# Token-wise attention of a fused transformer kernel: two serial passes of eight tiles become one pipeline of sixteen

## The chip, the cores and the metric

The kernel runs on one core of a Trainium2 chip. The metric is the device time of one launch in microseconds (us). The core has a tensor engine (PE; its weight loads are shown as PEld), a vector engine (DVE), a scalar engine (ACT), GpSimd (POOL) and a sync engine (SP). They run their own instruction streams and meet only in semaphores.

## The reference, cut to what matters

The whole program is a chain of attention, feed-forward and mixture-of-experts layers on a stream of 4 x 512 tokens with 128 features, all in fp32. The change concerns one of them, the first layer of the second block. It is an attention inside one token: the 16 heads of a token attend to each other, with 8 features a head.

```python
# B, S, DM, H = 4, 512, 128, 16
Q = (x @ Wq.T).reshape(b, s, h, hd)
K = (x @ Wk.T).reshape(b, s, h, hd)
V = (x @ Wv.T).reshape(b, s, h, hd)
scores = jnp.einsum('bshd,bstd->bsht', Q, K) / math.sqrt(hd)
attn = jax.nn.softmax(scores, axis=-1)
out = jnp.einsum('bsht,bstd->bshd', attn, V).reshape(b, s, dm)
return out @ Wfc.T
...
x = x + _L1_attn_a_ref(_layernorm(x, axis=-1), Wq, Wk, Wv, Wfc)
```

Each token needs 16 x 16 scores of 8 products each, so a tile of 128 tokens (one token to a partition) has 2048 products to a partition for the scores and 2048 for the values.

## The kernel before

The program is cut into stages, and between two stages all engines meet: each drains and counts up `batch_done`, SP clears the semaphores and counts up `batch_go`. The stage in question is the fifth, called "c" in the code. The windowed attention with its feed-forward part comes before it, the experts after it.

Before the change the stage is a loop over two halves of the stream (`Fori(0, NP)`), of 8 token tiles each (`PAIR`). A half copies its rows from `X` to `XB`, norms them (`layer_norm`, whose inverse root is taken by POOL, L1879), and writes `Y`. PE turns four tiles at a time (L318) and projects them to queries, keys and values, 384 columns a tile (L734); ACT copies these out of PSUM into `c_qkv`. Then DVE goes through the tiles `u`:

- `scores(u)`: the products of queries and keys (L1674, 2048 elements), their sums over the 8 features (L1678), the maximum of each head (L1679), the subtraction (L1680). ACT takes the exponential (L1169).
- `weights(u)`: the sum of the exponentials (L1685), the reciprocal (L1686), the multiplication of the 256 weights (L1687), which releases POOL.
- POOL multiplies weights and values (L2036, 2048 elements).
- `summed(u)`: DVE sums these products over the 16 heads (L1691) into `c_os`.

DVE issues them as scores(u), summed(u-2), weights(u-1). Every DVE step waits for the step before it through `after`. At the end of a half PE turns the sums (L318) and applies the output matrix (L741), and DVE adds the result to the rows (L1707). All tiles of the stage are fp32 and lie in one buffer, `arena`; `small` holds the maxima, sums and reciprocals, `ps` is PSUM with 8 banks.

In the lines printed here, `part` and `full` are views, `tt` is `dve.tensor_tensor`, and `wide` repeats an operand along an axis. `need(engine, sem, n)` waits only if n is above zero.

Of the kernel before, what the change touches and what calls it, by code (L numbers as in the profile page):

```python
# [21 lines left out]
P = 128  # L22
# [89 lines left out]
def program(nc, x_in, w_in, c_in, r_in, out, scratch, c_at):  # L112
# [3 lines left out]
    with ExitStack() as ctx:  # L116
# [35 lines left out]
        def carve(n):  # L152
# [62 lines left out]
        c_qkv = carve(PAIR * 384).rearrange("p (j n) -> p j n", j=PAIR)  # L215
        c_prod = carve(2048)
        c_mix = carve(2 * 2048).rearrange("p (z n) -> p z n", z=2)
        c_sc = carve(2 * 256).rearrange("p (z h t) -> p z h t", z=2, h=HB)
        c_e = carve(2 * 256).rearrange("p (z h t) -> p z h t", z=2, h=HB)
        c_os = carve(PAIR * P)  # L220
        c_oT = carve(512)

# [31 lines left out]
            c_xT_ps c_xT c_proj c_qkv_in c_shift c_exp c_wts c_prod c_red c_sum c_os_in c_oT_ps c_oT_in c_out  # L254
# [58 lines left out]
        def _(pe):  # L313
# [412 lines left out]
            def head_attention(ln):  # L726
                pe.wait_ge(s.ln_out, ln)
                for z in range(2):
                    transposes(0, lambda j: Y[:, NT * z + j, :]).then_inc(s.c_xT_ps, 1)
                    pe.wait_ge(s.c_xT, z + 1)  # L730
                    if z:
                        pe.wait_ge(s.c_qkv_in, z)
                    for j in range(NT):
                        last = mm(ps[:, 1 + j, 0:384], xT[:, j * P:(j + 1) * P], W("c_qkv"), start=True, stop=True)  # L734
                    last.then_inc(s.c_proj, 1)
                for z in range(2):
                    pe.wait_ge(s.c_os_in, z + 1)
                    transposes(0, lambda j: c_os[:, (NT * z + j) * P:(NT * z + j + 1) * P]).then_inc(s.c_oT_ps, 1)
                    pe.wait_ge(s.c_oT_in, z + 1)
                    for j in range(NT):  # L740
                        last = mm(ps[:, 5 + z, j * P:(j + 1) * P], c_oT[:, j * P:(j + 1) * P], W("c_fc"),  # L741
                                  start=True, stop=True)
                    last.then_inc(s.c_out, 1)

# [115 lines left out]
            def stages(which):  # L860
                ln = 0
                for i, st in enumerate(which):
                    if st == "c":
                        ln += 1
                        head_attention(ln)
# [24 lines left out]
            if STAGES >= 5:  # L890
                with pe.Fori(0, NP) as b:
                    pe.wait_ge(batch_go, b + 5)
                    pe.sem_inc(batch_seen, 1)
                    stages(["c"])
                    pe.drain().then_inc(batch_done, 1)
            if STAGES >= 6:
                pe.wait_ge(batch_go, NP + 5)
                pe.sem_inc(batch_seen, 1)
                experts(0)
            if STAGES >= 7:  # L900
                with pe.Fori(0, NB) as b:
                    pe.wait_ge(batch_go, b + NP + 6)
# [3 lines left out]
            if STAGES >= 8:  # L906
                pe.wait_ge(batch_go, NB + NP + 6)
# [7 lines left out]
        def _(act):  # L915
# [243 lines left out]
            def head_attention():  # L1159
                for z in range(2):  # L1160
                    act.wait_ge(s.c_xT_ps, z + 1)
                    copy(xT[:, :], ps[:, 0, :]).then_inc(s.c_xT, 1)
                    act.wait_ge(s.c_proj, z + 1)
                    copy(c_qkv[:, NT * z:NT * z + NT, :], ps[:, 1:1 + NT, 0:384]).then_inc(s.c_qkv_in, 1)
                for u in range(PAIR):
                    act.wait_ge(s.c_shift, u + 1)
                    if u >= 2:
                        act.wait_ge(s.c_prod, u - 1)
                    act.activation(c_e[:, u % 2], c_sc[:, u % 2], ACT.Exp, scale=float(HD) ** -0.5)\  # L1169
                        .then_inc(s.c_exp, 1)  # L1170
                for z in range(2):
                    act.wait_ge(s.c_oT_ps, z + 1)
                    copy(c_oT, ps[:, 0, :]).then_inc(s.c_oT_in, 1)
# [88 lines left out]
            if STAGES >= 5:  # L1262
                with act.Fori(0, NP) as b:
                    act.wait_ge(batch_go, b + 5)
                    act.sem_inc(batch_seen, 1)
                    steps_done.n = 0
                    stages(["c"])
                    act.drain().then_inc(batch_done, 1)
            if STAGES >= 6:
                act.wait_ge(batch_go, NP + 5)  # L1270
# [3 lines left out]
            if STAGES >= 7:  # L1274
                with act.Fori(0, NB) as b:
                    act.wait_ge(batch_go, b + NP + 6)
# [4 lines left out]
            if STAGES >= 8:  # L1281
                act.wait_ge(batch_go, NB + NP + 6)
# [8 lines left out]
        def _(dve):  # L1291
# [374 lines left out]
            def head_attention():  # L1666
                part = lambda u, n: c_qkv[:, u, 128 * n:128 * n + 128].rearrange("p (h d) -> p h d", h=HB)
                full = [P, HB, HB, HD]

                def scores(u):  # L1670
                    b = u % 2
                    dve.wait_ge(s.c_qkv_in, u // NT + 1)
                    prod = c_prod.rearrange("p (h t d) -> p h t d", h=HB, t=HB)
                    after(tt(prod, part(u, 0).unsqueeze(2).broadcast_to(full),  # L1674
                             part(u, 1).unsqueeze(1).broadcast_to(full), ALU.mult))
                    if u >= 2:
# [648 lines left out]
```

## Time and profile before

| | us |
|---|---|
| median of the runs before (2257.24 to 2271.3) | 2269.24 |
| the profiled execution, its own time | 2261.32 |
| its span, first to last instruction | 2259.5 |
| stage "c" within it, from 1566.18 to the first instruction of the next stage at 1802.24 | 236.06 |

Over the span PE is busy 72%, DVE 58%, ACT 48% and POOL 39%, and TensorE's granted clock is 0.846 of full speed. These are means over eight stages with different limits; what this change does is read from its own stage.

### The profile page before, as it was taken

The numbers are of one execution on the slowest core, as the hardware profiler recorded it, in microseconds if no ns is written. First come the engines' busy times: TensorE is split into PE (matmuls) and PEld (weight loads), VectorE is DVE, ScalarE is ACT, GpSimd is POOL, SyncE is SP. The second block draws the span as 40 slices with busy tenths as digits, with TensorE's granted clock in tenths as the row PEclk, the third lists the DMA queues.
The fourth block names the chain that finished last, engine by engine and source line by source line (L and its number), as shares of the span: only waits on it lengthen the run. The fifth ranks groups of instructions, "written<-read, shape, count | busy, mean of one in ns | idle before, by whom it ended". The sixth has DMA issues, their size and how long they took to land. (4 is left out here: it accounts for less than half of the span.)

```text
span 2259.5 us, 37774 instructions
## 1 busy us (share of the span) xinstructions
PE 1630.8 (72%) x13344; PEld 1160.5 (51%) x13344; DVE 1318.2 (58%) x3740; ACT 1083.2 (48%) x2727; POOL 874.8 (39%) x628
## 2 busy tenths in 40 slices
PE   6999996889988568988868998884011166455586
PEld 5888883666666333445436666662010055344464
DVE  3454545886776245567568777752968745433344
ACT  3565664877787245654347778762000022222132
POOL 1232234766665013244366666640544402100102
PEclk9999998999999868998779999997555578777578
DMA  4000000111111000000001111100000001000001
GB/s 178 1 1 1 1 1 12 30 27 24 28 30 22 6 0 1 1 1 2 1 20 27 27 26 29 24 20 5 0 0 0 0 1 38 0 0 0 0 4 53
DMA packets 31073, 36.43 MB, mean 16 GB/s; under 512 B 19120, under 2 KB 21168, under 8 KB 30512
## 3 DMA queue, kind: packets, MB, share of 16 engines
q1 hardware_dynamic: 29872, 32.01, 5.4%
q8 instruction: 106, 1.74, 0.3%
q0 software_dynamic: 1024, 2.10, 0.3%
q14 instruction: 71, 0.58, 0.1%
HBM read 12.08 MB, written 3.15 MB: 7 GB/s over the span
## 5 line engine op out<-in xcount | busy, mean ns | idle before, releaser
L918 ACT ACTIVATE arena<-ps 128x512 f32<-128x512 f32 (+5 forms) x684 | 373.8, 606 | 297.9 <-PE ps L318 143.1
L318 PE MATMUL ps<-consts,arena 128*128 128x128 f32 x416 | 89.1, 362 | 296.4 <-DVEq L1695 139.8
L318 PEld LDWEIGHTS ps<-consts,arena 128*128 128x128 f32 x416 | 61.1, 181 | 328.1 <-DVEq L1695 141.6
L1053 ACT ACTIVATE arena<-arena,g_small 128x128 f32<-128x128 f32 x512 | 199.0, 404 | 0.5
L1153 ACT ACTIVATE arena<-ps 128x320 f32<-128x320 f32 (+4 forms) x256 | 132.5, 561 | 137.4 <-PE ps L676 134.6
L1460 DVE CUSTOM_DVE_ANT_0 arena<-ps,consts,g_ss 128x128 f32<-128x128 f32 x512 | 145.6, 347 | 77.1 <-PE ps L482 72.2
L1962 POOL TENSOR_TENSOR arena<-arena,consts 128x512 f32<-128x512 f32 (+1 forms) x64 | 92.9, 1452 | 194.3 <-ACT arena L1153 194.2
L1983 POOL TENSOR_TENSOR arena<-arena 128x512 f32<-128x512 f32 x64 | 82.1, 1282 | 183.8 <-DVE arena L1468 183.7
L2036 POOL TENSOR_TENSOR arena<-arena 128x2048 f32<-128x2048 f32 x16 | 109.5, 6842 | 99.9 <-DVE arena L1687 99.9
L676 PE MATMUL ps<-arena 32*128 32x160 f32 (+4 forms) x1024 | 119.9, 454 | 21.1 <-ACT arena L1153 10.5
L1879 POOL TENSOR_TENSOR rstd<-rstd,consts 128x4 f32<-128x4 f32 (+2 forms) x16 | 28.8, 1798 | 262.4 <-DVE rstd L1317 219.9
L1467 DVE TENSOR_TENSOR arena<-ps,tabs 128x512 f32<-128x512 f32 x128 | 87.7, 685 | 50.7 <-ACT arena L1022 44.8
L1993 POOL TENSOR_TENSOR g_ss<-g_ss,consts 128x8 f32<-128x8 f32 x64 | 105.4, 1647 | 7.1
L1805 DVE SCALAR_TENSOR_TENSOR arena<-ps,arena 128x128 f32<-128x128 f32 x256 | 72.1, 344 | 61.8 <-PE ps L850 60.3
L1402 DVE TENSOR_REDUCE arena<-arena 128x8 f32<-128x1032 f32 x32 | 39.3, 1228 | 115.7 <-ACT arena L976 115.7
L583 PE MATMUL ps<-arena,weights 128*128 128x512 f32 (+1 forms) x192 | 101.4, 639 | 6.0 <-ACT arena L1082 4.1
L676 PEld LDWEIGHTS ps<-arena 32*128 32x128 f32 x1024 | 60.8, 204 | 87.4 <-ACT arena L1153 53.9
L1996 POOL TENSOR_TENSOR g_ss<-g_ss,consts 128x8 f32<-128x8 f32 x64 | 104.7, 1636 | 0.0
L1053 ACT ACTIVATION_READ_ACCUMULATOR arena<-arena,g_small 128x1 f32 x512 | 103.8, 203 | 0.0
L1909 POOL TENSOR_TENSOR arena<-arena,consts 128x8 f32<-128x8 f32 x32 | 52.6, 1645 | 124.2 <-DVE arena L1402 124.2
L2052 POOL DMA_INDIRECT sorted_rows<-arena,e_idx x32 | 30.9, 967 | 169.6 <-DVE arena L1805 162.3
L1986 POOL TENSOR_TENSOR arena<-arena 128x512 f32<-128x512 f32 x64 | 81.4, 1271 | 38.8 <-issue 35.2
(249 smaller groups left out, 4287.2 us busy)
## 6 DMA issues: line engine op xcount, KB each, us to landing
arena<-arena SPq DMA_DIRECT2D x112, 128.0 KB, 2.3
weights<-in_w SPq DMA_DIRECT2D x1, 5069.0 KB, 24.0
weights<-in_w SPq DMA_DIRECT2D x1, 2052.0 KB, 12.5
arena<-Y SPq DMA_DIRECT2D x16, 128.0 KB
arena<-Y SPq DMA_DIRECT2D x16, 127.0 KB
consts<-in_c SPq DMA_DIRECT2D x1, 1278.0 KB, 8.6
out<-X SPq DMA_DIRECT2D x1, 1024.0 KB, 5.1
sorted_rows<-arena,e_idx POOLq DMA_INDIRECT x32
```

The costliest lines, as they stand in the source:

```text
L318: last = tr(ps[:, bank, j * P:(j + 1) * P], src(j), ident)
L583: mm(ps[0:m, 4 + c % 2, :], W("f_w1", at, at + m), g_hnT, start=True, stop=True)\
L676: last = mm(ps[:, 2 * (st % 2) + hh, 0:n], b_kT[rows, k % 2, r, j * P:(j + 1) * P], b_qT[rows, k % 2, j * P:j * P + n], start=True, stop=True)
L918: copy = lambda o, i: act.activation(o, i, ACT.Copy)
L1053: last = act.activation(g_p[:, n % 2, 4 * hf + i, :], g_sc[:, 4 * hf + i, :], ACT.Exp, scale=-1.0, bias=g_mn[:, h:h + 1], accum_out=g_rs[: ...
L1153: act.activation(b_p[:, U % 2, 2 * gp:2 * gp + 2, at:at + n], ps[:, b:b + 2, 0:n], ACT.Exp, scale=float(HD) ** -0.5).then_inc(s.b_exp, 1)
L1460: last = dve.tensor_tensor_reduce(g_sc[:, 4 * hf + i, :], ps[:, 4 + hf, i * P:(i + 1) * P], C("mask_f" if n % NT else "mask_f0"), g_ss[:, ...
L1467: tt(heads(low[0]), heads(src), table(tabs_at), ALU.mult)
L1962: pool.tensor_tensor(v, v, m.unsqueeze(1).broadcast_to([P, NG, n]), ALU.mult)\
L1993: stepped_after(pool.tensor_tensor(ss[:, 8:16], ss[:, 8:16], C("neghalf", 0, 8), ALU.pow))
L1996: pool.tensor_tensor(ss[:, 0:8], ss[:, 0:8], C("neghalf", 0, 8), ALU.pow).then_inc(gs.root, 1)
L2036: pool.tensor_tensor(c_mix[:, u % 2].rearrange("p (h d t) -> p h d t", h=HB, t=HB), c_e[:, u % 2].unsqueeze(2).broadcast_to(full), vals.un ...
```

## The change

The loop over halves is gone; one pipeline goes over the 16 tiles of the stream (`TT`), and norms four tiles at a time as it comes to them, straight from `X`. For each tile:

- The queries stay in PSUM. ACT copies only keys and values (256 columns) to `c_kv`.
- DVE's product (`products`, L1707 of the new file) reads queries from PSUM and keys from SBUF, and writes them feature by feature: 8 planes of 256.
- PE adds the 8 planes: 8 matmuls of 256 columns with the identity as weights, accumulated in PSUM (`sum_products`, L740). The maximum and the subtraction (`shift`) read PSUM.
- The weights are no longer divided. POOL multiplies the exponentials as they are with the values. DVE sums these into PSUM (L1734) and multiplies the 128 sums by the reciprocals (L1735).
- DVE's order is products(t), sums(t-1), values(t-2), shift(t), and at some steps four rows of norm or the addition of an output.

```diff
             def head_attention():
-                part = lambda u, n: c_qkv[:, u, 128 * n:128 * n + 128].rearrange("p (h d) -> p h d", h=HB)
-                full = [P, HB, HB, HD]
-
-                def scores(u):
-                    b = u % 2
-                    dve.wait_ge(s.c_qkv_in, u // NT + 1)
-                    prod = c_prod.rearrange("p (h t d) -> p h t d", h=HB, t=HB)
-                    after(tt(prod, part(u, 0).unsqueeze(2).broadcast_to(full),
-                             part(u, 1).unsqueeze(1).broadcast_to(full), ALU.mult))
-                    if u >= 2:
-                        dve.wait_ge(s.c_exp, u - 1)
-                    after(dve.tensor_reduce(c_sc[:, b], prod, AX, ALU.add))
-                    after(dve.tensor_reduce(mxa[:, :], c_sc[:, b], AX, ALU.max))
-                    tt(c_sc[:, b], c_sc[:, b], wide(mxa[:, :], [P, HB, HB], 2), ALU.subtract).then_inc(s.c_shift, 1)
...
+                heads = lambda ap: ap.rearrange("p (h d) -> p d h", h=HB)
+                full = [P, HD, HB, HB]
+
+                def products(u):
+                    dve.wait_ge(s.c_kv, u + 1)
+                    need(dve, s.c_s, u - 1)
+                    tt(c_prod[:, u % 2].rearrange("p d (h t) -> p d h t", h=HB),
+                       heads(ps[:, u % 2, 0:128]).unsqueeze(3).broadcast_to(full),
+                       heads(c_kv[:, u % 4, 0:128]).unsqueeze(2).broadcast_to(full), ALU.mult).then_inc(s.c_prod, 1)
+
+                def shift(u):
+                    dve.wait_ge(s.c_s, u + 1)
+                    need(dve, s.c_mix, u - 1)
...
+                    sc = ps[:, 2 + u % 2, 0:256].rearrange("p (h t) -> p h t", h=HB)
+                    after(dve.tensor_reduce(mxa[:, :], sc, AX, ALU.max))
+                    tt(c_e[:, u % 2], sc, wide(mxa[:, :], [P, HB, HB], 2), ALU.subtract).then_inc(s.c_shift, 1)
+
+                def sums(u):
+                    r = c_sums[:, u % 2, :]
                     dve.wait_ge(s.c_exp, u + 1)
...
+                    after(dve.tensor_reduce(r, c_e[:, u % 2], AX, ALU.add))
+                    dve.reciprocal(r, r).then_inc(s.c_sum, 1)
+
+                def values(u):
+                    z, j = u // NT, u % NT
+                    dve.wait_ge(s.c_mix, u + 1)
+                    dve.wait_ge(s.c_sum, u + 1)
...
+                    red = ps[:, 7, 0:P]
+                    need(dve, s.c_os, u)
+                    after(dve.tensor_reduce(red, c_mix[:, u % 2].rearrange("p (n t) -> p n t", t=HB), AX, ALU.add))
+                    tt(c_os[:, z % 2, j, :].rearrange("p (h d) -> p h d", h=HB), red.rearrange("p (h d) -> p h d", h=HB),
+                       wide(c_sums[:, u % 2, :], [P, HB, HD], 2), ALU.mult).then_inc(s.c_os, 1)
+
+                for t in range(-5, TT + 4):
+                    if 0 <= t < TT:
+                        products(t)
+                    if 0 <= t - 1 < TT:
+                        sums(t - 1)
+                    if 0 <= t - 2 < TT:
+                        values(t - 2)
+                    if 0 <= t < TT:
+                        shift(t)
+                    z, r = (t + 5) // NT, (t + 5) % NT
+                    if z < NB and r == 0:
+                        norm_stats(0, X[:, NT * z:NT * z + NT, :])
+                        norm_var(0)
+                    if z < NB and r == 1:
+                        norm_apply(0, Y[:, NT * z:NT * z + NT, :], X[:, NT * z:NT * z + NT, :], gs.ln)
+                    if t >= 7 and (t - 7) % NT == 0:
+                        z = (t - 7) // NT
+                        x = X[:, NT * z:NT * z + NT, :]
+                        dve.wait_ge(s.c_out, z + 1)
+                        tt(x, x, ps[:, 6, :].rearrange("p (j d) -> p j d", j=NT), ALU.add).then_inc(s.c_add, 1)
```

PE and POOL, cut to the new parts (PE's loop is turn_x, project(t+1), sum_products(t), rows_out):

```diff
+                def project(u):
+                    z, j = u // NT, u % NT
+                    pe.wait_ge(s.c_xT, z + 1)
+                    need(pe, s.c_prod, u - 1)
+                    mm(ps[:, u % 2, 0:384], c_xT[:, z % 2, j * P:(j + 1) * P], W("c_qkv"), start=True, stop=True)\
+                        .then_inc(s.c_qkv, 1)
+
+                def sum_products(u):
+                    pe.wait_ge(s.c_prod, u + 1)
+                    need(pe, s.c_shift, u - 1)
+                    for d in range(HD):
+                        last = mm(ps[:, 2 + u % 2, 0:256], ident, c_prod[:, u % 2, d, :], start=d == 0, stop=d == HD - 1)
+                    last.then_inc(s.c_s, 1)
...
+                def mix(u):
+                    pool.wait_ge(s.c_exp, u + 1)
+                    need(pool, s.c_os, u - 1)
...
+                for t in range(-5, TT + 1):
+                    z, r = (t + 5) // NT, (t + 5) % NT
+                    if 0 <= t - 1 < TT:
+                        mix(t - 1)
+                    if z < NB and r == 0:
+                        pool.wait_ge(gs.var, rooted.next())
+                        pool.tensor_tensor(g_rstd[:, 0, :], g_rstd[:, 0, :], C("neghalf", 0, NT), ALU.pow)\
+                            .then_inc(gs.root4, 1)
```

DVE in the middle of a half, before (one tile, from its query-key product to the next one):

```order
L1674 TENSOR_TENSOR arena<-arena 128x2048
L1678 TENSOR_REDUCE arena<-arena 128x256
L1679 TENSOR_REDUCE small<-arena 128x16
L1680 TENSOR_TENSOR arena<-arena,small 128x256
L1691 TENSOR_REDUCE arena<-arena 128x128
L1685 TENSOR_REDUCE small<-arena 128x16
L1686 RECIPROCAL small<-small 128x16
L1687 TENSOR_TENSOR arena<-arena,small 128x256
L1674 TENSOR_TENSOR arena<-arena 128x2048
```

DVE now, at step t = 4, the tile after which four rows of the third group are normed (L1377 is the application of the norm, four instructions):

```order
L1707 TENSOR_TENSOR arena<-ps,arena 128x2048
L1724 TENSOR_REDUCE c_sums<-arena 128x16
L1725 RECIPROCAL c_sums<-c_sums 128x16
L1734 TENSOR_REDUCE ps<-arena 128x128
L1735 TENSOR_TENSOR arena<-ps,c_sums 128x128
L1717 TENSOR_REDUCE small<-ps 128x16
L1718 TENSOR_TENSOR arena<-ps,small 128x256
L1377 TENSOR_SCALAR Y<-X,mv,g_rstd 128x128 x4
L1707 TENSOR_TENSOR arena<-ps,arena 128x2048
```

The reduction of 2048 products (L1678) and the product with the reciprocals (L1687) are gone from between two query-key products, and a product of 128 elements (L1735) has come; the subtraction stands last, right ahead of the norm where there is one.

PE before, one half:

```order
L318 MATMUL ps<-consts,Y 128x128 x4
L734 MATMUL ps<-weights,xT 128x384 x4
L318 MATMUL ps<-consts,Y 128x128 x4
L734 MATMUL ps<-weights,xT 128x384 x4
L318 MATMUL ps<-consts,arena 128x128 x4
L741 MATMUL ps<-weights,arena 128x128 x4
```

PE now, from the start of the stage:

```order
L319 MATMUL ps<-consts,Y 128x128 x4
L733 MATMUL ps<-weights,arena 128x384 x2
L740 MATMUL ps<-arena,consts 128x256 x8
L319 MATMUL ps<-consts,Y 128x128 x4
L733 MATMUL ps<-weights,arena 128x384
L740 MATMUL ps<-arena,consts 128x256 x8
L733 MATMUL ps<-weights,arena 128x384
L740 MATMUL ps<-arena,consts 128x256 x8
```

The projections, which stood in two blocks ahead of a half, now stand one by one, each ahead of the 8 matmuls that add the products of a tile.

## Rows read from the trace of the kernel before

**Rows 1.** Stage "c": length, busy us of PE, PEld, DVE, ACT, POOL; clock, DMA share, GB/s.
```profile
1566.18:1802.24 236.06, 31.58 (x96) 20.22 (x96) 180.38 (x186) 19.18 (x30) 112.76 (x18) 0.55 0.00 0
```

**Rows 2.** Timeline of one period of a half: start, length, engine, line.
```profile
1604.63 7.34 POOL L2036 TENSOR_TENSOR arena<-arena 128x2048 f32<-128x2048 f32 x1 [3.87 <-DVE arena L1687]
1606.79 2.29 DVE L1678 TENSOR_REDUCE arena<-arena 128x256 f32<-128x2048 f32 x1
1609.11 0.42 DVE L1679 TENSOR_REDUCE small<-arena 128x16 f32<-128x256 f32 x1
1609.57 2.69 DVE L1680 TENSOR_TENSOR arena<-arena,small 128x256 f32<-128x256 f32 x1
1612.18 2.27 DVE L1691 TENSOR_REDUCE arena<-arena 128x128 f32<-128x2048 f32 x1
1612.29 0.42 ACT L1169 ACTIVATE arena<-arena 128x256 f32<-128x256 f32 x1 [10.80 <-DVE arena L1680]
1614.60 0.42 DVE L1685 TENSOR_REDUCE small<-arena 128x16 f32<-128x256 f32 x1
1615.06 0.25 DVE L1686 RECIPROCAL small<-small 128x16 f32<-128x16 f32 x1
1615.34 0.43 DVE L1687 TENSOR_TENSOR arena<-arena,small 128x256 f32<-128x256 f32 x1
1615.68 2.29 DVE L1674 TENSOR_TENSOR arena<-arena 128x2048 f32<-128x2048 f32 x1
1615.85 7.35 POOL L2036 TENSOR_TENSOR arena<-arena 128x2048 f32<-128x2048 f32 x1 [3.87 <-DVE arena L1687]
```

**Rows 3.** Timeline of the end of the second half.
```profile
1788.59 5.33 POOL L2036 TENSOR_TENSOR arena<-arena 128x2048 f32<-128x2048 f32 x1 [3.71 <-DVE arena L1687]
...
1798.26 2.08 PE L741 MATMUL ps<-weights,arena 128*128 128x128 f32 x8 [0.69 <-ACT arena L918]
1800.37 0.69 DVE L1707 TENSOR_TENSOR XB<-XB,ps 128x512 f32<-128x512 f32 x1 [3.19 <-PE ps L741]
```

**Rows 4.** DVE lines of other stages: count, shortest/median/longest ns, first and last start.
```profile
L1467 DVE TENSOR_TENSOR arena<-ps,tabs x128: 676/682/693, 367.4 to 1489.4; 128x512 f32<-128x512 f32 x128
L1495 DVE RECIPROCAL g_small<-g_small x64: 189/190/203, 395.6 to 1516.3; 128x8 f32<-128x8 f32 x64
L1343 DVE TENSOR_SCALAR Y<-X,mv,g_rstd x64: 333/341/1361, 13.0 to 1242.1; 128x128 f32<-128x128 f32 x64
```

**Rows 5.** Timeline in the second windowed stage: four norm instructions of DVE, one POOL product.
```profile
1240.41 1.80 DVE L1343 TENSOR_SCALAR Y<-X,mv,g_rstd 128x128 f32<-128x128 f32 x3
...
1240.58 1.31 POOL L1983 TENSOR_TENSOR arena<-arena 128x512 f32<-128x512 f32 x1 [1.23 <-DVE arena L1468]
```

**Rows 6.** Matmuls by line and shape: busy us, mean ns of one record.
```profile
L422 PE MATMUL ps<-arena 128*128 128x256 f32 x64 | 19.0, 379 | 0.0
```

**Rows 7.** Timeline: PE in the second half's projections, and in the experts' stage.
```profile
1692.95 5.43 PE L734 MATMUL ps<-weights,xT 128*128 128x384 f32 x8 [0.69 <-ACT xT L918]
...
1863.00 1.02 PE L841 MATMUL ps<-arena,weights 128*128 128x512 f32 x2
```

**Rows 8.** Timeline of the start of the first half.
```profile
1566.91 1.64 DVE L1312 BATCH_NORM_STATS2 stats<-XB 128x6 f32<-128x128 f32 x8
...
1569.51 1.65 POOL L1879 TENSOR_TENSOR rstd<-rstd,consts 128x8 f32<-128x8 f32 x1 [26.59 <-DVE rstd L1317]
1571.19 2.14 DVE L1320 TENSOR_SCALAR Y<-XB,mv,rstd 128x128 f32<-128x128 f32 x8 [1.76 <-POOL rstd L1879]
1573.39 1.12 PE L318 MATMUL ps<-consts,Y 128*128 128x128 f32 x4 [8.46 <-DVE Y L1320]
...
1575.20 4.58 PE L734 MATMUL ps<-weights,xT 128*128 128x384 f32 x8 [0.69 <-ACT xT L918]
```

**Rows 9.** PE's busy time and granted clock in 2 us stretches of the small heads' stage.
```profile
1004.00:1006.00 2.00, 0.48 (x8) 1.00 0.00 0
1006.00:1008.00 2.00, 1.06 (x10) 1.00 0.00 0
```

More of the change, by code:

```diff
@@ L742, in head_attention @@
                                   start=True, stop=True)
                     last.then_inc(s.c_out, 1)
+                for t in range(-3, TT + 3):
+                    z = (t + 3) // NT
+                    if (t + 3) % NT == 0 and z < NB:
+                        turn_x(z)
+                    if 0 <= t + 1 < TT:
+                        project(t + 1)
+                    if 0 <= t < TT:
+                        sum_products(t)
+                    if t >= 6 and (t - 6) % NT == 0:
+                        rows_out((t - 6) // NT)
@@ L890, in _ @@
             if STAGES >= 5:
[L891 to L895, printed above, removed]
+                pe.wait_ge(batch_go, 5)
+                pe.sem_inc(batch_seen, 1)
+                head_attention()
+                pe.drain().then_inc(batch_done, 1)
             if STAGES >= 6:
-                pe.wait_ge(batch_go, NP + 5)
+                pe.wait_ge(batch_go, 6)
                 pe.sem_inc(batch_seen, 1)
@@ L1159, in head_attention, with keep_kv, exps @@
             def head_attention():
[L1160 to L1165, printed above, removed]
-                    act.wait_ge(s.c_shift, u + 1)
-                    if u >= 2:
[L1168 to L1173, printed above, removed]
+                def keep_kv(u):
+                    act.wait_ge(s.c_qkv, u + 1)
+                    need(act, s.c_mix, u - 3)
+                    copy(c_kv[:, u % 4, :], ps[:, u % 2, 128:384]).then_inc(s.c_kv, 1)
+                def exps(u):
+                    act.wait_ge(s.c_shift, u + 1)
+                    act.activation(c_e[:, u % 2], c_e[:, u % 2], ACT.Exp, scale=float(HD) ** -0.5).then_inc(s.c_exp, 1)
+                for t in range(-3, TT + 3):
+                    z = (t + 3) // NT
+                    if (t + 3) % NT == 0 and z < NB:
+                        act.wait_ge(s.c_xT_ps, z + 1)
+                        need(act, s.c_qkv, NT * (z - 1))
+                        copy(c_xT[:, z % 2, :], ps[:, 4, :]).then_inc(s.c_xT, 1)
+                    if 0 <= t + 1 < TT:
+                        keep_kv(t + 1)
+                    if t >= 6 and (t - 6) % NT == 0:
+                        z = (t - 6) // NT
+                        act.wait_ge(s.c_oT_ps, z + 1)
+                        need(act, s.c_out, z)
+                        copy(c_oT, ps[:, 5, :]).then_inc(s.c_oT, 1)
+                    if 0 <= t < TT:
+                        exps(t)
             def full_attention():
@@ L1262, in _ @@
             if STAGES >= 5:
[L1263 to L1268, printed above, removed]
+                act.wait_ge(batch_go, 5)
+                act.sem_inc(batch_seen, 1)
+                steps_done.n = 0
+                head_attention()
+                act.drain().then_inc(batch_done, 1)
             if STAGES >= 6:
-                act.wait_ge(batch_go, NP + 5)
+                act.wait_ge(batch_go, 6)
                 act.sem_inc(batch_seen, 1)
@@ L2161, in _ @@
             if STAGES >= 5:
-                with sp.Fori(0, NP) as b:
-                    sp.wait_ge(batch_done, 4)
-                    clear()
+                sp.wait_ge(batch_done, 4)
+                clear()
             if STAGES >= 6:
```

138 lines of the change are left out of this document (54 added, 84 removed).

## The prediction

> **What bounds the kernel now.** I read the stage's busy times first. Stage "c" lasts 236.1 us; DVE is busy 180.4 us of it, POOL 112.8, PE 31.6 [rows 1]. DVE looks like the bound at 76%, but part of its busy time is waiting. That shows in the timeline of one period [rows 2]: POOL's product L2036 starts at 1604.63 and the next at 1615.85, so a tile costs 11.2 us. Within it POOL and DVE's two-input steps take turns. L1680 is a subtraction of 256 elements; its like L1687 takes 0.43 us, but L1680 takes 2.69 and ends as POOL ends (1612.26 against 1611.97). The product L2036 takes 5.33 us where DVE has nothing to do [rows 3] and 7.34 here, because it starts while L1674 still runs. The reductions L1678 and L1679 run beside POOL at full speed (2.29, 0.42). So a DVE instruction with two SBUF inputs and a POOL product exclude each other, a reduction does not. The loop of waits is: weights (L1687) -> POOL waits for L1674, then works -> L1680 can end -> L1691, L1685, L1686, L1687. POOL itself is idle 3.87 us of the 11.2.
>
> Which DVE instructions are exempt decides much of the change. L1467, a product with one input in PSUM, never takes over 0.69 us in 128 instances, and L1495, a reciprocal, never over 0.20 in 64, in stages in which POOL works beside them. But the norm's L1343, which reads SBUF alone, goes from 0.34 to 1.36 us [rows 4]. How it happens is seen in the timeline [rows 5]: POOL slips in between two of the four instructions of a norm, and the next one waits until POOL is done (three of them take 1.80 us).
>
> **One step of the new pipeline.** DVE's own work: product 2.29 (as L1674, same size), sum of exponentials 0.42, reciprocal 0.25, value sums 2.29 (as L1691), product with the reciprocals about 0.30 (estimated from 0.69 for 512 and 0.43 for 256 elements), maximum 0.42, subtraction 0.42: 6.4 us, some 6.2 with the overlap of independent neighbours (L1674 starts 0.09 before L1687 ends) [rows 2, 3]. The reduction L1678 (2.29), the product L1687 (0.43) and the wait in L1680 (2.27) are gone.
>
> PE's new work is 8 fp32 matmuls of 256 columns. A record of 256 columns takes 0.379 us [rows 6], two overlapping ones of 512 take 1.02 [rows 7]; from the two, a column costs 0.835 ns and the tail of a burst 0.165 us. Each matmul is two records (L734: 4 matmuls, x8), so 16 records at 0.214 are 3.4 us, with the tail 3.6. At the lower clock L734's eight records of 384 took 5.43 us [rows 7]: 1.71 ns a column, twice as much, and 16 records of 256 take 7.0 with their tail.
>
> The step's path: product 2.29, to PE 0.06 (L1320 ends 1573.33, L318 starts 1573.39 [rows 8]), sums 3.6, back 0.05, maximum and subtraction 0.8: 6.8 us. Between product and maximum DVE does 3.3 us of other work, so it waits 0.3 for PE; PE is the bound by a little. Behind that wait stands the next product, and PE waits for that one: the two engines take turns on the path. POOL: its exponentials come 0.55 us after the subtraction (ACT 0.42, and two hand-overs), its product takes 5.33 and must be done when values(t) begins, 6.8 + 3.0 us after that subtraction: 4 us of slack. All DVE products of the step have a PSUM input, so I price the exclusion within a step at nothing; if it were not so, POOL would start 2.3 us late and the reciprocal, if it too had to wait, would stand until 7.6 us into the step; with the value sums and shift() behind it, that is an 11.2 us step. ACT's copy of keys and values is off the path, one step ahead. On PE, the projection (two records of 384, 0.8) and every fourth step the turning of the rows and the output matrix (about 2.3 with ACT's copy) fit into the 3.2 us between PE's end and the next product's end; without that cover they cost up to 2.3 us, three times.
>
> **The sum**, from the start of the stage:
> - To the first product: statistics of four tiles, half of 2.60 (from L1312 to L1879); inverse root 1.65; norm 1.1; turning 1.12; ACT's copy 0.6; projection at the lower clock 1.3 and its tail; ACT 0.4; hand-overs [rows 8]. 8.0.
> - 16 steps of 6.8: 108.8.
> - Norms within the pipeline: statistics after t = 3 and 7 (1.4 each), application after t = 0, 4, 8 (1.1 each): 6.1. Additions at t = 7, 11, 15, 0.7 each [rows 3]: 2.1.
> - **Port stalls**: each application stands right behind shift(t). POOL is released 0.55 us after the subtraction, as the third of four norm instructions runs. As before [rows 5] the next one then waits for the whole POOL product: 5.33 less what runs beside it, 5.2, three times: 15.6. The bounds are 0 (POOL comes after the fourth has begun) and 16.5.
> - [...] A burst that begins after a rest keeps that level for long: the eight projections of one half took 5.43 us [rows 7], those of the other 4.58 [rows 8]. So in the one the clock rose only at the end, in the other some 3.7 us into the burst, 5.5 after the turning had begun. I take 5 us: 2.5 us worth of work is done by then, the remaining 0.9 at full rate; 5.9 instead of 3.4, so 2.5 a restart. Restarts: the first tile, and the one behind each stall (over 9 us of rest): 4 x 2.5 = 10.0. Within steady steps PE rests 2.4 us and works 4.2. The clock stayed full through 4 us with 1.54 busy in another stage [rows 9]; I take the full level here.
> - Tail: after the last subtraction POOL is done at 5.95, value sums and product 2.6, turning 1.2, copy 0.65, output matrix 2.1, addition 0.7 [rows 3, 8]: 13.3; to the next stage 0.4.
>
> Together 164.3 against 236.1: 71.8 less. The profiled execution's own time is 2261.3, so 2189.5; the median of the runs stands 7.9 above that execution. I take half of it: **2193**.
>
> [...] The change reads queries and keys with a step of 8 elements, 32 bytes; before, both were read in rows of 8 neighbours. The row nearest to it is POOL's: L2036 reads the values with that step already and takes 5.33 us for 2048 elements [rows 3], 2.6 ns each, as L1983, which reads runs of 32 neighbours, takes 1.31 for 512 [rows 5]. So POOL pays nothing for it here; DVE has no such SBUF read in the trace. If DVE paid, I bound it by nothing below and POOL's 5.33 above.
> [...]
>
> **Rivals.**
> 1. *The lower clock stays* (17%). The steady burst is short, with a rest in each step. A step is then 2.29 + 0.06 + 7.0 + 0.05 + 0.8 = 10.2; 16 of them cost 54 more, the 10 of restarts fall away: 2237. For it: the stage's 0.55 now. Against it: the stretch that kept the full clock [rows 9], and that at the lower clock PE would work over 8 of 10.2 us, which should lift it; so a mixture, near 2215, is as likely as the whole.
> 2. *No stalls* (17%). The four norm instructions are through before POOL asks (they start 0.27 apart, 1.1 in all; POOL asks at 0.55, so it needs luck). 15.6 and three restarts (7.5) fall away: 2170.
> 3. *The stepped reads are slow* (13%). At 4.5 us a product, between the bounds, a step is 9.0: +35, 2228; at 5.33 it is 2242.
> 4. *The exclusion holds for PSUM inputs and reciprocals too* (3%): steps of 11.2 us, +70, stalls and restarts partly inside: 2250. The lines that never stretch speak against it [rows 4].
> 5. *Slower than before* (3%): the accumulating matmuls do not overlap, each record waits for the tail of the one before, at the lower clock. 16 x (0.43 + 0.17) = 9.6, a step of 12.8; 16 of them are 205 and 45.5 for the rest without restarts: 250, 14 more than now and 86 more than forecast: 2279. It decides from a step of 11.9 us on, that is 8.7 us of PE. Against it: records overlap [rows 6, 7].
> That the change does not do what it says is shut out by the order of instructions.
>
> **Chances.** Forecast 47%, from 2178 to 2212 with the uncertain terms (stalls, restarts, 0.3 us a step). For 8 in 10 the range must take in rivals 2 and most of 1 and 3: 2160 to 2240. A measurement of this kernel tells about 1% (23 us) from no change. Faster by over 1% is all but rival 5, part of 4 and the ends of 1 and 3: 0.95; within 1% 0.03; slower 0.02.
>
> **What the new profile would show.** Right: a period of 6.8 us between DVE's 2048-element products, with DVE waiting some 0.3 us for PE before the maximum; the subtraction at 0.42 us, never 2.7; POOL's product at 5.33 throughout; the norm application stretched to over 6 us at t = 0, 4, 8; a granted clock near 1 between them; 164 us for the stage, other stages unchanged. Wrong: a product over 2.3 us (rival 3), PE's burst at 7 us throughout (rival 1), no norm instruction over 0.4 us (rival 2). What I may have missed: a cost of writing value sums to PSUM (no such DVE write in the trace; priced as L1691), and DVE's extra waits on semaphores, five ahead of the value sums, priced at nothing because they stand behind running work; each tenth of a microsecond there costs 1.6 us.

## The result, and the profile after

| | before | after |
|---|---|---|
| median of 4 runs each, same chip (us) | 2270.27 (2257.24 to 2275.85) | 2242.86 (2237.58 to 2247.2) |
| the profiled execution, its own time | 2261.32 | 2247.2 |
| stage "c" in it | 236.06 | 209.45 |
| everything else in its span | 2023.4 | 2035.9 |

The changed kernel takes 0.9898 of the time before, 95% interval 0.9867 to 0.9929: 23 us less, between 16 and 30. The prediction was 76 less, and the time lies just above the range that was given. The stage itself became 26.6 us shorter; 71.8 were forecast. What surrounds the stage was not changed. It varies in single executions of the kernels of this study between 2013 and 2046 us, so I read the mechanism from the stage, and kernels against each other from their medians.

The stage as a whole, and one steady step cut into pieces (columns as in [rows 1]):

```profile
1562.20:1771.65 209.45, 116.30 (x352) 85.28 (x352) 150.17 (x169) 17.54 (x41) 91.14 (x20) 0.73 0.00 0
1607.50:1611.60 4.10, 0.00 (x1) 0.00 (x0) 4.10 (x3) 0.69 (x2) 3.29 (x1) 1.00 0.00 0
1611.60:1612.60 1.00, 0.99 (x5) 0.89 (x6) 0.97 (x3) 0.00 (x0) 1.00 (x1) 0.99 0.00 0
1612.60:1613.60 1.00, 1.00 (x4) 0.82 (x3) 1.00 (x1) 0.00 (x0) 1.00 (x1) 0.50 0.07 16
1613.60:1614.60 1.00, 1.00 (x4) 0.82 (x3) 0.96 (x2) 0.00 (x0) 0.15 (x1) 0.50 0.00 0
1614.60:1615.60 1.00, 1.00 (x4) 0.73 (x4) 0.06 (x1) 0.00 (x0) 0.00 (x0) 0.50 0.00 0
1615.60:1616.60 1.00, 1.00 (x5) 0.86 (x4) 0.00 (x0) 0.00 (x0) 0.00 (x0) 0.81 0.00 0
1616.60:1617.60 1.00, 1.00 (x4) 0.40 (x3) 0.51 (x2) 0.00 (x0) 0.00 (x0) 1.00 0.00 0
```

PE rests 4.10 us with the clock granted in full, starts its burst in full, and has worked for about a microsecond when the granted clock goes to half (0.50 of full speed). It comes back only toward the end of the burst. The slices hold some 3.4 us at the lower level (three whole ones, and 0.4 of the one that reads 0.81); half of that is 1.7, which is what this burst of 5.41 us takes over the one of 3.72 us in the same stage. The same step in the timeline, from one product of DVE to the next burst of PE (it answers to [rows 2]):

```profile
1597.54 3.85 DVE L1707 TENSOR_TENSOR arena<-ps,arena 128x2048 f32<-128x2048 f32 x1
...
1601.45 5.41 PE L740 MATMUL ps<-arena,consts 128*128 128x256 f32 x16 [4.10 <-DVE arena L1707]
...
1606.90 0.42 DVE L1717 TENSOR_REDUCE small<-ps 128x16 f32<-128x256 f32 x1 [2.41 <-PE ps L740]
1607.36 0.42 DVE L1718 TENSOR_TENSOR arena<-ps,small 128x256 f32<-128x256 f32 x1
1607.70 3.86 DVE L1707 TENSOR_TENSOR arena<-ps,arena 128x2048 f32<-128x2048 f32 x1
...
1608.31 5.45 POOL L2088 TENSOR_TENSOR arena<-arena 128x2048 f32<-128x2048 f32 x1 [4.70 <-ACT arena L1192]
...
1611.61 5.41 PE L740 MATMUL ps<-arena,consts 128*128 128x256 f32 x16 [4.11 <-DVE arena L1707]
```

L1707 is now the query-key product. The ring is the forecast one: product, burst, maximum and subtraction, next product. Its size is not: the product takes 3.86 us where 2.29 was forecast, the burst 5.41 where 3.6 was. The step is 10.16 us, not 6.8. By line over the whole stage (columns: busy us, mean ns of one, idle before):

```profile
L740 PE MATMUL ps<-arena,consts 128*128 128x256 f32 x256 | 90.0, 528 | 54.3 <-DVE arena L1707 54.3
L2088 POOL TENSOR_TENSOR arena<-arena 128x2048 f32<-128x2048 f32 x16 | 87.2, 5447 | 95.1 <-ACT arena L1192 95.1
...
L1707 DVE TENSOR_TENSOR arena<-ps,arena 128x2048 f32<-128x2048 f32 x16 | 61.7, 3856 | 2.6 <-ACT arena L942 2.6
L1734 DVE TENSOR_REDUCE ps<-arena 128x128 f32<-128x2048 f32 x16 | 36.2, 2265 | 2.2 <-POOL arena L2088 2.2
...
L1717 DVE TENSOR_REDUCE small<-ps 128x16 f32<-128x256 f32 x16 | 6.8, 425 | 47.1 <-PE ps L740 47.1
```

DVE idles 47.1 us of the stage for PE, and PE 54.3 us for DVE: neither is the bound, they take turns. Of the 16 bursts, seven take 5.41 us, seven between 5.7 and 6.6, one 5.22, one 3.72; together 90.0. The sum of the prediction had 16 x 3.6 + 10 for restarts, 67.6. The norm at t = 4:

```profile
1629.21 6.12 DVE L1377 TENSOR_SCALAR Y<-X,mv,g_rstd 128x128 f32<-128x128 f32 x4
...
1629.82 5.43 POOL L2088 TENSOR_TENSOR arena<-arena 128x2048 f32<-128x2048 f32 x1 [3.98 <-ACT arena L1192]
```

Four instructions that take 1.12 us at the start of the stage take 6.12, because POOL's product begins between two of them. This happens three times, as forecast.

### The profile page after: what moved, and what is told of

Its sections match the earlier page's. It is cut to its first block and busy times, and to the rows that moved or that the text cites. A ratio compares the mean times of both kernels' runs of the same rounds, so it can differ in the third digit from the quotient of the medians.

```text
span 2245.4 us, 38321 instructions
## 1 busy us (share of the span) xinstructions
PE 1731.9 (77%) x13600; PEld 1238.6 (55%) x13600; DVE 1285.8 (57%) x3722; ACT 1081.9 (48%) x2738; POOL 855.0 (38%) x630
## 3 DMA queue, kind: packets, MB, share of 16 engines
q0 software_dynamic: 1024, 2.10, 0.3%
## 5 line engine op out<-in xcount | busy, mean ns | idle before, releaser
L942 ACT ACTIVATE arena<-ps 128x512 f32<-128x512 f32 (+4 forms) x700 | 376.4, 595 | 327.7 <-PE ps L319 173.5
L2031 POOL TENSOR_TENSOR arena<-arena 128x512 f32<-128x512 f32 x64 | 82.1, 1283 | 183.5 <-DVE arena L1502 183.5
L740 PE MATMUL ps<-arena,consts 128*128 128x256 f32 x256 | 90.0, 528 | 54.3 <-DVE arena L1707 54.3
L2088 POOL TENSOR_TENSOR arena<-arena 128x2048 f32<-128x2048 f32 x16 | 87.2, 5447 | 95.1 <-ACT arena L1192 95.1
L1927 POOL TENSOR_TENSOR rstd<-rstd,consts 128x4 f32<-128x4 f32 (+1 forms) x14 | 25.5, 1822 | 240.0 <-DVE rstd L1351 197.6
L740 PEld LDWEIGHTS ps<-arena,consts 128*128 128x128 f32 x256 | 68.9, 275 | 80.5 <-DVE arena L1707 65.8
L1855 DVE SCALAR_TENSOR_TENSOR arena<-ps,arena 128x128 f32<-128x128 f32 x256 | 72.1, 344 | 61.7 <-PE ps L875 60.8
L319 PE MATMUL ps<-consts,Y 128*128 128x128 f32 x128 | 26.1, 340 | 100.1 <-DVE Y L1354 56.5
```

The costliest lines, as they stand in the source:

```text
L319: last = tr(ps[:, bank, j * P:(j + 1) * P], src(j), ident)
L740: last = mm(ps[:, 2 + u % 2, 0:256], ident, c_prod[:, u % 2, d, :], start=d == 0, stop=d == HD - 1)
L942: copy = lambda o, i: act.activation(o, i, ACT.Copy)
```

## The experiments

The theory behind them: (A) the product is slow because it reads the keys in SBUF with a step of 8 elements, and the longer product is also what makes PE rest long enough to lose its clock; (B) PE's clock would fall anyway, since bursts are short; (C) the product is slow because one input is in PSUM. Each kernel is the changed one with the edit shown. "Stage" is the length of "c" in its profiled execution.

| kernel | edit | median us (runs) | over before, same chip, 95% | stage us | product us | PE bursts, sum us |
|---|---|---|---|---|---|---|
| changed | – | 2242.86 (4) | 0.9898 (0.9867–0.9929) | 209.45 | 3.86 | 90.0 |
| perm | queries and keys feature-major | 2204.05 (4) | 0.9758 (0.9720–0.9795) | 165.73 | 2.28 | 71.5 |
| perm_k | keys only | 2193.88 (1) | – | 174.72 | 2.28 | 80.5 |
| norm_early | norm ahead of the subtraction | 2216.47 (4) | 0.9808 (0.9776–0.9841) | 186.24 | 3.86 | 84.9 |
| fill8 | PE kept busy behind its burst | 2226.23 (4) | 0.9856 (0.9792–0.9920) | 194.33 | 3.87 | 70.8 |
| perm_delay | perm, DVE 1.64 us later | 2220.31 (1) | – | 205.45 | 2.28 | 86.2 |
| k_step4 | keys with a step of 4 | 2238.82 (1) | – | 213.57 | 4 x 1.06 | 91.8 |
| k_step2 | keys with a step of 2 | 2200.52 (1) | – | 171.83 | 2 x 1.22 | 76.5 |
| perm_norm | perm and norm_early | 2175.45 (4) | 0.9620 (0.9579–0.9662) | 148.19 | 2.28 | 72.1 |
| ahead | product(t+1) ahead of the subtraction(t) | 2194.57 (5) | 0.9677 (0.9642–0.9713) | 159.48 | 3.88 | 71.5 |
| perm_norm_ahead | all three | 2151.4 (4) | 0.9504 (0.9461–0.9547) | 133.35 | 2.29 | 64.4 |

### The layout of queries and keys: perm and perm_k

The columns of the two weight matrices are laid out on the host in the order feature, head. Every feature of the 16 heads is then 16 neighbours, and the results are the same numbers.

```diff
+                rows = lambda ap: ap.rearrange("p (d h) -> p d h", h=HB)
...
-                       heads(ps[:, u % 2, 0:128]).unsqueeze(3).broadcast_to(full),
-                       heads(c_kv[:, u % 4, 0:128]).unsqueeze(2).broadcast_to(full), ALU.mult).then_inc(s.c_prod, 1)
+                       rows(ps[:, u % 2, 0:128]).unsqueeze(3).broadcast_to(full),
+                       rows(c_kv[:, u % 4, 0:128]).unsqueeze(2).broadcast_to(full), ALU.mult).then_inc(s.c_prod, 1)
...
-        "c_qkv": side([c["Wq"].T, c["Wk"].T, c["Wv"].T]), "c_fc": c["Wfc"].T,
+        "c_qkv": side([c["Wq"].T.reshape(D, HB, HD).transpose(0, 2, 1).reshape(D, D), c["Wk"].T.reshape(D, HB, HD).transpose(0, 2, 1).reshape(D, D), c["Wv"].T]), "c_fc": c["Wfc"].T,
```

> The columns of the query and key weights are laid out feature by feature on the host, so that the product (L1707 of the changed kernel) reads both operands in runs of neighbours; nothing else changes. Theory: the step of 8 elements costs the product 1.57 us (3.86 instead of 2.29). Then the product is 2.29 us again, PE is released 1.57 us earlier in each of 16 steps, and stage c falls from 209.4 us by up to 25, to about 184. Rival: it is the PSUM operand or the sheer size that makes it slow; then the product stays at 3.86 and the stage at 209. Second rival: the step pays it back to PE, because a shorter step changes nothing in PE's clock or makes it worse: product at 2.29 but the stage at 195 or more.

In perm_k only the keys (the line with `c_kv` and the columns of `Wk`) are changed; the queries in PSUM are still read with a step of 8, each of them 16 times in a row.

> Only the keys are laid out feature by feature; the queries are still read from PSUM with the step, each of them repeated 16 times. Theory: what costs is a new address with every element, and only the keys have that, so the product is 2.29 us as with both. Rival: a step in PSUM costs as well, or the two add up: a product between 2.4 and 3.86.

The timeline of perm at three of its steps, then its product (count, shortest/median/longest ns, first and last start), then the same line of perm_k:

```profile
1608.63 2.28 DVE L1708 TENSOR_TENSOR arena<-ps,arena 128x2048 f32<-128x2048 f32 x1
...
1610.96 3.72 PE L740 MATMUL ps<-arena,consts 128*128 128x256 f32 x16 [2.53 <-DVE arena L1708]
...
1642.58 3.72 PE L740 MATMUL ps<-arena,consts 128*128 128x256 f32 x16 [2.53 <-DVE arena L1708]
...
1680.82 5.41 PE L740 MATMUL ps<-arena,consts 128*128 128x256 f32 x16 [2.53 <-DVE arena L1708]
```
```profile
L1708 DVE TENSOR_TENSOR arena<-ps,arena x16: 2277/2280/2291, 1577.7 to 1715.2; 128x2048 f32<-128x2048 f32 x16
```
```profile
L1708 DVE TENSOR_TENSOR arena<-ps,arena x16: 2278/2279/2293, 1574.7 to 1721.2; 128x2048 f32<-128x2048 f32 x16
```

With rows of neighbours the product is back at 2.28 us, a PSUM input or not, so (C) falls. The keys alone do it: the step of the queries in PSUM costs nothing here. PE now rests 2.53 us ahead of a burst in a steady step. Eight of the 16 bursts take 3.72 us, where the changed kernel had one, and the step is then 6.89; the other eight take 4.78 to 5.53 us, two of them after the same rest of 2.53 us. The stage is 43.7 us shorter than in the changed kernel: 16 x 1.575 = 25.2 from the product and 90.0 - 71.5 = 18.5 from the bursts, together 43.7. Only the 25 had been expected, the bursts had not. Their share is the less certain one: perm_k has the same product and the same rests, but its bursts add up to 80.5 us instead of 71.5, and its stage is 9.0 us longer. So in single executions of one schedule the bursts can differ by as much as that.

### What makes PE's clock fall: fill8 and perm_delay

fill8 leaves the stepped read as it is and gives PE something to do behind each burst, eight matmuls into a corner of PSUM that nobody reads:

```diff
                     last.then_inc(s.c_s, 1)
+                    for _ in range(8):
+                        mm(ps[:, 5, 0:256], ident, W("c_qkv", 0, 256), start=True, stop=True)
```

> PE gets 8 more matmuls of 256 columns behind the sums of each tile, into a bank that is free then, with constant operands; their results are not used. Theory: the clock falls in the middle of each burst (PE rests 4.1 us before it), and a fuller PE keeps it: a burst of 16 records takes 3.6 us in steady steps instead of 5.4, the granted clock of the stage rises from 0.73 to over 0.9, and the stage falls by 13 times 1.8, to about 186, if the filler (3.4 us) fits into PE's rest. Rival: the burst is slow for another reason (accumulation, or the read of the products beside DVE and POOL): bursts stay at 5.4 and the stage at 209 or more.

```profile
1611.49 0.40 DVE L1726 TENSOR_REDUCE c_sums<-arena 128x16 f32<-128x256 f32 x1
1611.61 3.72 PE L740 MATMUL ps<-arena,consts 128*128 128x256 f32 x16 [0.69 <-DVE arena L1709]
```

The slow product stays (3.87 us), the burst takes 3.72 and the step 8.5. The medians of the two kernels are too close to part them (the intervals of the ratios overlap), so this is read from the stage: it gets 15.1 us shorter although PE has twice as many of these matmuls to do, and lies 28.6 above perm, of which the product is 25.4. Eleven of its 16 bursts take 3.6 or 3.7 us, and PE rests 0.69 us ahead of them in a steady step. The bursts give back 19.2 us and the stage only 15.1 (some 186 us had been expected): at three tiles PE turns the sums and applies the output matrix, and there the filler delays the next burst by 0.9 to 1.5 us behind its product. perm_delay is the opposite: the product is fast, and a reduction of 1440 constants, which nobody uses, makes DVE later by what the stepped read had cost.

```diff
+                    dve.tensor_reduce(small[:, 4, :], W("a_qkv", 0, 16 * 90).rearrange("p (n t) -> p n t", t=90), AX, ALU.add)
                     tt(c_prod[:, u % 2].rearrange("p d (h t) -> p d h t", h=HB),
```

> As perm, with the product fast at 2.29 us, but a reduction of 1440 constants (1.57 us from start to next start) ahead of each product, whose result is not used. So the step's timing is that of the changed kernel while no stepped read is left. Theory: the slow product costs twice, once in itself (25 us) and once because PE then rests 4.1 us and its clock falls inside every burst (18.5 us); with the delay the bursts are 5.4 us again, steps 10.15 us, and the stage is at about 209. Rival: bursts are slow because PE reads while the stepped product or its traffic runs; then they stay at 3.7 with the delay, and the stage is at 191.

```profile
1607.82 1.64 DVE L1707 TENSOR_REDUCE small<-weights 128x16 f32<-128x1440 f32 x1
...
1609.38 2.28 DVE L1709 TENSOR_TENSOR arena<-ps,arena 128x2048 f32<-128x2048 f32 x1
...
1611.72 5.41 PE L740 MATMUL ps<-arena,consts 128*128 128x256 f32 x16 [4.09 <-DVE arena L1709]
```

Without any stepped read the slow burst of 5.41 us is back as soon as PE's rest is 4.09 us, and so are the step of 10.14 and nearly the whole stage (205.45). So it is when PE works and rests, and not the data, that costs the clock. (B) falls as well, since half of the bursts of perm, as short, run at the full level. But the length of one rest doesn't decide alone. Of the 18 bursts behind a rest of 4.09 to 4.11 us (changed, norm_early, perm_delay) all are slow, 5.36 us or more. Of the 24 behind 2.52 to 2.59 us (perm, perm_k, k_step2, perm_norm) 14 take 3.72 us and ten 5.15 to 5.41. And in the changed kernel a rest of 1.84 us was followed by a burst of 3.72, one of 1.85 us by a burst of 5.41.

### How the stepped read is priced: k_step4 and k_step2

The keys of a tile are laid out so that the product is four instructions of 512 elements with a step of 4 elements, or two of 1024 with a step of 2. The number of products and the planes are the same; the queries lie and are read as in perm, in k_step2 too, other than its expectation says. For k_step4 (k_step2 has 2 in the place of 4):

```diff
+                    for k in range(4):
+                        to = c_prod[:, u % 2].rearrange("p (g s) n -> p s g n", s=4)[:, k].rearrange("p g (h t) -> p g h t", h=HB)
+                        q = rows(ps[:, u % 2, 0:128]).rearrange("p (g s) h -> p s g h", s=4)[:, k]
+                        ks = c_kv[:, u % 4, 0:128].rearrange("p (g h s) -> p s g h", s=4, h=HB)[:, k]
+                        part = [P, HD // 4, HB, HB]
+                        last = tt(to, q.unsqueeze(3).broadcast_to(part), ks.unsqueeze(2).broadcast_to(part), ALU.mult)
```

> [...]

> The keys lie so that the product reads them with a step of 2 elements (8 bytes), in two instructions of 1024 elements each; queries, planes and all else as in the changed kernel. A step of 8 and one of 4 elements both cost about 0.75 ns an element over a contiguous read. [...] Theory B, any step but 1 costs in full: 1.93 us an instruction, 3.86 a tile, about 2240 us again. Theory C, at a step of 2 nothing is paid: 1.16 us an instruction, a stage near 170 us.

By line, first k_step4, then k_step2 (busy us, mean ns of one):

```profile
L1713 DVE TENSOR_TENSOR arena<-ps,arena 128x512 f32<-128x512 f32 x64 | 64.0, 1063 | 2.6 <-ACT arena L942 2.6
```
```profile
L1713 DVE TENSOR_TENSOR arena<-ps,arena 128x1024 f32<-128x1024 f32 x32 | 37.5, 1215 | 2.6 <-ACT arena L942 2.6
```

From 2048 neighbours in 2.281 us and 256 in 0.425 I estimate 1.04 ns for an element and 0.16 us for an instruction. At no cost of the step, 512 elements should then take 0.69 us, and at the price of the step of 8 (0.77 ns more for each element) 1.08. With a step of 4 they take 1.06, 0.73 ns more for each element. With a step of 2, 1024 elements should take 1.22 us at no cost and take 1.215: nothing more. I had put half of the price down as possible too; theory C of that run, no cost, was right. So the cost does not grow in proportion to the step: 0 at 2, 0.73 ns at 4, 0.77 at 8. No run shows why. The stages follow the product, 213.57 and 171.83 us.

### The stalls of the norm: norm_early and perm_norm

The four norm instructions go from behind the subtraction to ahead of it, where DVE waits for PE anyway and, in a step of 10 us, POOL is through with the tile before:

```diff
+                    z, r = (t + 5) // NT, (t + 5) % NT
+                    if z < NB and r == 1:
+                        norm_apply(0, Y[:, NT * z:NT * z + NT, :], X[:, NT * z:NT * z + NT, :], gs.ln)
                     if 0 <= t < TT:
                         shift(t)
```

> Four instructions of the norm's application stand ahead of shift(t) instead of behind it; nothing else changes. Theory: behind the subtraction they collide with POOL's product (6.12 us for four instead of 1.12); ahead of it POOL is idle and DVE waits 2.4 us for PE anyway, so they cost nothing: three times 6.1 us go, and part of the slow bursts behind them (6.2 instead of 5.4 us, 2 in all): the stage at about 190. Rival: POOL's product of the step before still runs there and the stall only moves: the four still take over 3 us and the stage stays above 200.

```profile
1625.28 0.29 DVE L1735 TENSOR_TENSOR arena<-ps,c_sums 128x128 f32<-128x128 f32 x1
1625.49 1.11 DVE L1377 TENSOR_SCALAR Y<-X,mv,g_rstd 128x128 f32<-128x128 f32 x4
1627.78 0.42 DVE L1717 TENSOR_REDUCE small<-ps 128x16 f32<-128x256 f32 x1 [1.19 <-PE ps L740]
```

The norm takes 1.11 us and lies wholly in the wait. The stage is 23.2 us shorter, which 15.0 of stalls, 5.1 in the bursts, and the norm's own 3 x 1.1 that is covered now make up to within 0.2.

> Both edits together: query and key columns feature by feature, and the norm's application ahead of shift(t). Theory: the two costs are separate (43.7 us and 23.2 us of the stage's 209.4), so the stage comes to about 143 to 146, a little over the sum because DVE now waits only 0.3 us for PE and the norm's 1.1 us is no longer hidden; steps at 6.9 us, bursts of PE at 3.7 almost throughout. Rival: the clock needs the density that the stalls do not allow anyway, or the collision with POOL comes back in the shorter step (POOL's product now ends just as the norm begins): norms of over 2 us, stage at 152 or more.

Both edits together give 148.19 us, 17.5 below perm and 2 above the expected range; two of the four norms are stretched a little (2.14 and 1.56 us), since the step is shorter and POOL's product of the tile before is still running.

### Taking the burst off the path: ahead and perm_norm_ahead

DVE takes the next product before it waits for PE. ACT's copy of the keys goes one tile further ahead for it.

```diff
-                    if 0 <= t < TT:
-                        products(t)
+                    if 0 <= t + 1 < TT:
+                        products(t + 1)
```
```diff
-                    if 0 <= t + 1 < TT:
-                        keep_kv(t + 1)
...
+                    if 0 <= t + 2 < TT:
+                        keep_kv(t + 2)
```

> The changed kernel, with only the order moved: DVE takes the product of tile t+1 ahead of the maximum and subtraction of tile t, and ACT's copy of keys and values two tiles ahead follows from that. Stepped reads and norms stay as they are. PE then has a whole DVE step to add the products, so that its burst, slow or not, stands beside DVE's work. Theory A (the burst is on the path because of the order): DVE alone sets the step, 3.86 + 0.42 + 0.25 + 2.27 + 0.3 + 0.84 = 7.9 us less overlaps, about 7.8 against 10.15; 16 x 2.35 = 37 less on the stage, near 170 us, and the kernel near 2205. Theory B (the stepped read and the low clock would cost the same in any order): steps stay at 10 us and the time near 2240.

```profile
1602.10 2.24 DVE L1734 TENSOR_REDUCE ps<-arena 128x128 f32<-128x2048 f32 x1
1604.37 0.29 DVE L1735 TENSOR_TENSOR arena<-ps,c_sums 128x128 f32<-128x128 f32 x1
1604.57 0.42 DVE L1717 TENSOR_REDUCE small<-ps 128x16 f32<-128x256 f32 x1
...
1609.27 5.41 PE L740 MATMUL ps<-arena,consts 128*128 128x256 f32 x16 [3.29 <-DVE arena L1707]
...
1612.23 0.41 DVE L1717 TENSOR_REDUCE small<-ps 128x16 f32<-128x256 f32 x1
...
1622.39 1.11 DVE L1377 TENSOR_SCALAR Y<-X,mv,g_rstd 128x128 f32<-128x128 f32 x4
...
1626.27 0.41 ACT L1192 ACTIVATE arena<-arena 128x256 f32<-128x256 f32 x1
1626.40 3.92 DVE L1707 TENSOR_TENSOR arena<-ps,arena 128x2048 f32<-128x2048 f32 x1 [2.90 <-ACT arena L942]
```

The burst at 1609.27 is a slow one and still running when the maximum starts at 1612.23, which does not wait: it needs the burst before. The order alone, with every stepped read and two bursts of 5.41 us still there, takes 50.0 us off the stage, more than the 37 expected: steps are 7.7 us and DVE never waits for PE in them. About half of the 13 us past the forecast is that the stalls shrank too, which I had not seen (3 x 2.1); the restart bursts of over 5.41 us, which stood on the path as well, may be some 3 more, and the rest is not traced. ACT now has the copy of the keys ahead of the exponential, and that copy waits for the rows just normed; so POOL is released 3.8 us late at these tiles, after the norm. DVE idles 2.9 us there instead of 5.0.

> As perm_norm, and DVE makes the product of tile t+1 before the maximum of tile t (ACT copies keys and values one tile earlier), so that PE adds while DVE works. Theory: in the changed kernel PE's burst is on the path because product, sums and maximum of a tile follow each other; one tile of distance takes it off, and the step falls from 6.9 to DVE's own 6.2 us; stage about 135. Rival: POOL (5.45 us a product, and exponentials that come 0.55 us late) or a clock that falls now that PE rests in another pattern becomes the limit: step at 6.9 or more, stage at 144 or more.

```profile
1616.43 2.28 DVE L1708 TENSOR_TENSOR arena<-ps,arena 128x2048 f32<-128x2048 f32 x1
...
1617.04 5.48 POOL L2089 TENSOR_TENSOR arena<-arena 128x2048 f32<-128x2048 f32 x1 [0.85 <-ACT arena L1192]
...
1622.17 0.42 DVE L1719 TENSOR_TENSOR arena<-ps,small 128x256 f32<-128x256 f32 x1
```

Its stage as a whole:

```profile
1563.69:1697.04 133.35, 87.70 (x352) 68.37 (x352) 110.70 (x168) 18.14 (x41) 91.12 (x20) 0.82 0.00 1
```

All three together: steps of 6.1 us, a stage of 133.35 us and a kernel 5.0% below the one before the change. DVE sets the step; POOL rests only 0.60 to 0.86 us between its products of 5.49 us in a steady step, so it would be the next bound.

## Why the prediction was wrong

**The step that failed** is the first term of "One step of the new pipeline": "product 2.29 (as L1674, same size)". L1674 read its keys in rows of 8 neighbours, the new product reads them with a step of 8, and it takes 3.86 us. I had put this case aside as rival 3 at 13%, with the time between nothing and POOL's 5.33; that POOL pays nothing for such a read (2.6 ns an element with the step and without [rows 3, 5]) was no evidence for DVE. The bounds held the measured value, the value taken was the lower one. This is a mis-sized term, and it was the decisive one: perm, where only it is put right, has a stage of 165.73 us against 164.3 in my sum.

**The second half of the miss hangs on it.** "Within steady steps PE rests 2.4 us ... I take the full level here" was right in the main for the step that I had forecast: in perm four of the six bursts behind 2.53 us of rest take 3.72 us, and all bursts together 71.5 against 67.6 in my sum. At 3.86 us a product PE rests 4.10, and each steady burst loses 1.7 us. I priced rival 3 and rival 1 as separate cases, and one starts the other: rival 3 at 3.86 us alone would have been 2193 + 25 = 2218; with the bursts' 22.4 over the sum (90.0 - 67.6) it is 2240, against 2242.86 measured. Together 47.5 of excess; the stage has 45.2, since other terms came in some 2 us lower.

**What held.** To the first product 7.7 us (8.0 forecast). Stalls: three, 5.0 each (5.2), at the places named. The subtraction at 0.42 us in all 16, never 2.7; but that sign could not fail, since POOL's product is over before the next subtraction (1603.61 against 1607.36), as it would have been in the forecast step. What rules rival 4 out is the product L1707, which has an input in PSUM: it takes 3.86 us at 1607.70 with POOL's product beside it from 1608.31 on, and 3.82 for the first tile with POOL idle. In perm_norm_ahead a subtraction too takes 0.42 us at 1622.17, while POOL's product runs until 1622.52. Value sums to PSUM 2.27 (2.29). The four restart bursts 5.75 to 6.34 us (5.9); three others of 6.05 to 6.52 us, behind statistics or an addition or, once, a plain rest of 4.11 us, were not forecast. The level that these bursts were priced at is seen in the kernel before: its granted clock reads 0.50 in every slice of 1 us from 1693 to 1698, nearly the whole burst of 5.43 us, and from 1575 to 1578 in the one of 4.58, then 0.64 and 1.00. POOL's product 5.45, 0.1 over forecast and with slack in the steps. Rival 2 did not come: the norm was cut at every one of the three places. Rival 5 is out: it needed bursts of 8.7 us or more to make the kernel slower, and the longest is 6.52.

**The price of the stepped read.** With the input in SBUF, DVE took 0.77 ns more for an element at a step of 8 elements (the changed kernel against perm), 0.73 at a step of 4 (k_step4) and nothing more at a step of 2 (k_step2). For the queries in PSUM, each repeated 16 times, there was no cost (2.279 us in perm_k, 2.280 in perm). The trace before held no such read by DVE, so the 2.29 us of the forecast had no row behind it in this respect; the value between the bounds was for a run to give.

**What stays open.** What in the read costs the time is not shown: there are three steps, 8, 4 and 2, and no run parts the step from what else changes with it. A stepped read of PSUM without repeats was not tried. What decides between a fast and a slow burst is open too: rests of 4.1 us were always followed by slow ones here, rests of 2.5 us by fast and slow ones, and no run separates the length of the rest from what PE did before it. With it stays open how much of the 18.5 us that perm gained in the bursts would come back in another execution; perm_k's are 9 us longer.

## What to carry to other kernels

When a layout is turned so that one engine's output suits another (planes for PE), look at what the turned side reads: lay out the weights on the host so that the innermost run is of neighbours, which cost nothing in the kernel and was worth 44 us of the stage, 1.4% of the kernel. Where two engines take turns in a ring, price them together: the time that one adds is rest for the other, and here PE paid for the longer rest (4.10 us instead of 2.53) with its clock, so 1.6 us more on DVE became 3.3 a steady step. And before such a ring is tuned, try to break it by order: taking the next tile's product ahead of the wait was worth more (50 us of stage) than making the product fast (44).

## What the runs showed that was not expected

- DVE, a fp32 product with 2048 elements: 2.28 us with neighbours in SBUF, 3.86 with a step of 8; a step of 2 added nothing (1.215 us for 1024), a step of 4 added 0.73 ns an element and one of 8 added 0.77.
- PE lost its clock inside a burst that it had begun at the full level, about a microsecond after a rest of 4.1 us had ended, not during the rest: the granted clock reads 1.00 through the rest and 0.50 from 1612.6 to 1615.6. All 18 bursts behind such a rest were slow; behind rests of 2.5 us 14 of 24 were fast.
- Eight useless fp32 matmuls a step made a stage shorter: 70.8 us of bursts instead of 90.0, and 15 us off the stage. For the kernel as a whole the medians don't show it.
